# Row scan between two recurrences: norm, way in and way back with channels on partitions

## What is computed

```python
def _L1_ffn_ref(x, W, V, gamma, beta):      # R1, and R2 with its own weights
    Wx = jnp.einsum('bti,hi->bth', x, W)
    ...
    def step(yt, wx_t):
        yt = jax.nn.sigmoid(wx_t + yt @ Vt)
        return (yt, yt)
def _L2_conv_ref(x, W):                     # SC
    rows = jnp.moveaxis(x, 1, 0)
    row0 = rows[0]
    def step(carry, row):
        new = row + jax.nn.relu(conv1d_same(carry, W))
        return (new, new)
    ...
t = t + _L1_ffn_ref(_ln_t(t), L1_ffn_W, ...)
x = x + _L2_conv_ref(_ln_c(x), L2_conv_W)
t = t + _L2_ffn_ref(_ln_t(t), L2_ffn_W, ...)
```

## Time and profile before

| | us |
|---|---|
| median of 3 runs | 560.86 (560.37 to 563.21) |
| the profiled execution, its own time | 561.55 |
| its span | 559.1 |
| busy PE, PEld | 432.0, 329.5 |
| busy DVE, ACT, POOL | 370.2, 236.3, 226.9 |
| chain that ended last, shares | PE 48%, DVE 37%, ACT 5%, POOL 5% |

### The profile page before, as it was taken

The page is one execution under the profiler, slowest core; times in us unless marked ns, Lnnn a source line. Parts: engine busy times, 40 slices in busy tenths (PEclk is TensorE's granted clock), DMA queues, the critical chain, the costliest instruction groups (busy, mean ns, idle before and its releaser), DMA issues.

```text
span 559.1 us, 8700 instructions
## 1 busy us (share of the span) xinstructions
PE 432.0 (77%) x3066; PEld 329.5 (59%) x3066; DVE 370.2 (66%) x1228; ACT 236.3 (42%) x569; POOL 226.9 (41%) x293
## 2 busy tenths in 40 slices
PE   2788868986897757995589976799589848809996
PEld 2456744663347634994389964498355737606664
DVE  4988597749795696007924477501978498398885
ACT  1497555412774554673510024476379634000000
POOL 2598185004582491000500005000359278029994
PEclk9999999678998998899569997799589996558999
DMA  8300000000000000000000000000000000001223
GB/s 162 79 2 1 1 1 1 1 2 0 1 1 1 2 0 1 1 1 2 0 2 2 1 1 1 1 1 1 2 0 2 1 1 1 1 0 20 38 40 56
DMA packets 34670, 6.03 MB, mean 11 GB/s; under 512 B 33713, under 2 KB 34369, under 8 KB 34626
## 3 DMA queue, kind: packets, MB, share of 16 engines
q1 hardware_dynamic: 34626, 5.46, 5.6%
HBM read 3.36 MB, written 2.10 MB: 10 GB/s over the span
## 4 chain that ended last, share of the span: by engine, by line
PE 48%; DVE 37%; ACT 5%; POOL 5%; issue 2%; DMA 1%; SPq 1%; DVEq 0%; POOLq 0%
PE psum L1360 7%; DVE moments L330 6%; DVE ab L742 6%; PE psum L1122 5%; PE psum L1121 5%; DVE ab L726 4%; PE psum L616 4%; PE psum L461 4%; PE psum L1533 3%; POOL z L392 2%; PE psum L627 2%; PE psum L586 2%; PE psum L1553 2%; PE psum L1538 2%; POOL gate L804 2%
## 5 line engine op out<-in xcount | busy, mean ns | idle before, releaser
L461 PE MATMUL psum<-ident,z 128*128 128x128 f32 x256 | 54.2, 354 | 34.5 <-POOL z L392 31.4
L461 PEld LDWEIGHTS psum<-ident,z 128*128 128x128 f32 x256 | 38.5, 182 | 61.9 <-POOL z L392 43.2
L586 PE MATMUL psum<-wp_L,z_t 64*128 64x320 f32 x384 | 66.1, 473 | 3.4 <-ACT z_t L370 2.1
L330 DVE BATCH_NORM_STATS2 moments<-x_cols 128x6 f32<-128x64 f32 x448 | 61.6, 211 | 0.3
L392 POOL TENSOR_TENSOR z<-z,stats 128x496 f32<-128x496 f32 (+1 forms) x35 | 36.8, 1052 | 58.6 <-DVE z L316 58.6
L370 ACT ACTIVATE z_t<-psum 128x512 f32<-128x512 f32 x56 | 40.0, 719 | 33.5 <-PE psum L461 33.4
L586 PEld LDWEIGHTS psum<-wp_L,z_t 64*128 64x128 f32 x384 | 33.2, 192 | 31.0 <-issue 27.6
L387 POOL MEMSET z<- 128x16 f32 x32 | 4.0, 126 | 112.2 <-DVE z L316 111.8
L1213 ACT ACTIVATE ab<-psum,mv 128x128 f32<-128x128 f32 x108 | 39.7, 368 | 19.0 <-PE psum L1122 8.9
L392 POOL TENSOR_TENSOR z<-x_cols,stats 128x512 f32<-128x512 f32 x21 | 22.0, 1048 | 62.9 <-DVE stats L336 62.5
L1122 PE MATMUL psum<-ab,R_vt 128*128 128x128 f32 x216 | 46.8, 300 | 0.0
(11 more groups left out here) (256 smaller groups left out, 912.9 us busy)
## 6 DMA issues: line engine op xcount, KB each, us to landing
x_cols<-in_x_dram SPq DMA_DIRECT2D x16, 128.0 KB, 2.8
out_dram<-x_cols SPq DMA_DIRECT2D x32, 64.0 KB, 1.9
par<-in_par_dram SPq DMA_DIRECT2D x1, 644.5 KB
w<-in_w_dram SPq DMA_DIRECT2D x4, 64.0 KB, 2.3
w<-in_w_dram SPq DMA_DIRECT2D x1, 256.0 KB, 2.7
mask<-in_mask_dram SPq DMA_DIRECT2D x1, 64.0 KB, 2.8
row<-in_row_dram SPq DMA_DIRECT2D x1, 3.3 KB
w_bias<-in_w_dram SPq DMA_DIRECT2D x1, 8.0 KB, 1.9
```

The costliest lines, as they stand in the source:

```text
L330: m = dve.bn_stats(moments[:, q, k:k + 2, :].rearrange("p k m -> p (k m)"), X4[:, SQ * q + s, g:g + 2, :].rearrange("p g c -> p c g"))
L461: m = pe.transpose(bank(b % 2)[:, k * N:(k + 1) * N], block_of(Z)(4 * b + k), ident[:, :])
L586: m = pe.matmul(bank(slot_bank(s) + h, 2 * 5 * C), ZT[rows, s, :], wp[l][rows, :, :], start=True, stop=True)
```

## The change

V1, V2 as whole-map turns, and the norm of SC in blocks, are gone. `XC` now holds x as (row in group, group, channel) from L0 on, so that a block is one transpose wide; L0 still reads the old order, and writes the new one only after all of it is read (`xb`). `cent` is the 32x32 matrix that subtracts the mean over channels, in four copies.

In R1, 32 transposes of x (`turn_x_pe`) are put between the chain of the batch statistics and the first steps, with copies to `XT` on ACT (four banks) and DVE (four banks). In the 16 steps that count, DVE adds each step's states to `XT` and writes `XS`, which is `XR` with (group, channel) on the partitions. The states are not turned back and L1298 is left out for R1.

After the last step PE forms the centred map with (column modulo 4, channel) on the partitions, in two halves of 16 matmuls; each takes 32 partitions to 32 partitions and 512 columns, four to a bank. ACT squares the banks, PE sums the squares over channels and, after root (ACT) and reciprocal (DVE), spreads the result over the channels again; DVE multiplies and writes `RIN`. The scan is the same. After it, PE turns the scanned rows by 32x32 tiles into the layout of `XS`, DVE adds them in eight instructions, and `rows_back_pe` and `rows_back_act` turn blocks back to `XC` in front of, and beside, the norm of R2. F3 writes its result to `XR`, and SP stores from there. POOL makes two more constants (`to_var`, `from_var`).

```diff
+        def x_of(L):
+            return blocks(L.src).rearrange("p g s c -> p s g c") if L is t0 else by_block(L.src)
...
+            if L is r2:
+                for b in range(Q // 2):
+                    rows_back_act(act, b)
             for u in range(LN_STEPS):
+                if L is r2 and u < Q // 2:
+                    rows_back_act(act, Q // 2 + u)
...
+        XT = SQR[:, :].rearrange("p (s n) -> p s n", s=S)
+        XS = XR[:, :].rearrange("p (s n) -> p s n", s=S)
+        XM = XR[:, :].rearrange("p (s n m) -> p s m n", s=S, m=G)
+        XT_BANKS = [0, 1, 2, 3, 4, 5, 6, 4]
+        BACK_BANKS = [4, 5, 6, 7, 2, 3, 4, 5]
+        def turn_x_pe(pe, b):
+            for s in range(4 * b, 4 * b + 4):
+                m = pe.transpose(bank(XT_BANKS[b])[:, s % 4 * N:(s % 4 + 1) * N], block_of(XC)(s), ident[:, :])
+            m.then_inc(v1.s["ps"], 1)
+        def turn_x_copy(eng, b):
+            eng.wait_ge(v1.s["ps"], v1.at["ps"] + b + 1)
+            dst, src = XT[:, 4 * b:4 * b + 4, :], bank(XT_BANKS[b]).rearrange("p (s n) -> p s n", s=4)
+            if b >= 4:
+                eng.tensor_copy(dst, src).then_inc(v1.s["dve"], 1)
+            else:
+                eng.activation(dst, src, ACT.Copy).then_inc(v1.s["act"], 1)
+        def rows_back_pe(pe, b):
+            pe.wait_ge(sc.s["done"], sc.at["done"] + G * (b // 4 + 1))
+            if b >= 6:
+                pe.wait_ge(v2.s["act"], v2.at["act"] + b - 5)
+            for s in range(4 * b, 4 * b + 4):
+                m = pe.transpose(bank(BACK_BANKS[b])[:, s % 4 * N:(s % 4 + 1) * N], XS[:, s, :], ident[:, :])
+            m.then_inc(v2.s["ps"], 1)
+        def rows_back_act(act, b):
+            act.wait_ge(v2.s["ps"], v2.at["ps"] + b + 1)
+            act.activation(XC[:, b * BANK:(b + 1) * BANK], bank(BACK_BANKS[b]), ACT.Copy)\
+                .then_inc(v2.s["act"], 1)
...
+            if L is r1:
+                turn_x_pe(pe, 0)
+                turn_x_pe(pe, 1)
...
+            if L is r1:
+                turn_x_pe(pe, 2)
+                turn_x_pe(pe, 3)
...
+            if L is r1:
+                for b in (4, 5, 6):
+                    turn_x_pe(pe, b)
...
+                    if L is r1 and r == 0 and k == 2:
+                        pe.wait_ge(v1.s["dve"], v1.at["dve"] + 1)
+                        turn_x_pe(pe, 7)
                     for n, h in enumerate(STREAM_ORDER[r]):
+                        if L is r1 and r == 0 and k < 2:
+                            pe.wait_ge(v1.s["act"], v1.at["act"] + 2 * h + k + 1)
...
+            if L is r1:
+                pe.wait_ge(L.s["x1"], L.at["x1"] + STREAMS * CHUNK)
+                for g in range(G):
+                    scan_turn(pe, 0, g).then_inc(sc.s["zt_ps"], 1)
...
+            if L is r1:
+                for b in range(4, 8):
+                    turn_x_copy(dve, b)
...
+                for k in range(CHUNK):
+                    for h in STREAM_ORDER[1]:
+                        dve.wait_ge(L.s[f"step_y{h}"], L.at[f"step_y{h}"] + WARM + k + 2)
+                        first = h * NS_N * CHUNK + k
+                        dve.tensor_tensor(
+                            XS.rearrange("p s n -> p n s")[:, bass.ds(first, NS_N, CHUNK), :],
+                            XT.rearrange("p s n -> p n s")[:, bass.ds(first, NS_N, CHUNK), :], chunks(Y, k + 1, h), ALU.add)\
+                            .then_inc(L.s["x1"], 1)
...
+        def scan_turn(pe, half, g):
+            rows = slice(g * C, (g + 1) * C)
+            for m in range(G):
+                i = pe.matmul(bank(g)[m * C:(m + 1) * C, :], cent[rows, rows],
+                              XM[rows, half * (S // 2):(half + 1) * (S // 2), m, :], start=True, stop=True)
+            return i
+        def scan_unit(t, half, g):
+            return t[:, (G * half + g) * HALF:(G * half + g + 1) * HALF]
+        def scan_square(act, half, g):
+            return act.activation(scan_unit(Z, half, g), bank(g), ACT.Square)
...
+        def scan_norm_pe(pe):
+            L = sc
+            def variances(half):
+                pe.wait_ge(L.s["zt"], L.at["zt"] + G * (half + 1))
+                if half:
+                    pe.wait_ge(L.s["z"], L.at["z"] + 1)
+                for k in range(G):
+                    for g in range(G):
+                        m = pe.matmul(bank(4)[g * C:(g + 1) * C, 0:N], to_var[:, k * C:(k + 1) * C],
+                                      scan_unit(Z, half, g)[:, k * N:(k + 1) * N], start=(k == 0), stop=(k == G - 1))
+                m.then_inc(L.s["var_ps"], 1)
+            def deviations(half):
+                pe.wait_ge(L.s["rstd"], L.at["rstd"] + half + 1)
+                for k in range(G):
+                    for g in range(G):
+                        if half and k == 0:
+                            pe.wait_ge(L.s["z"], L.at["z"] + g + 1)
+                        rows = slice(g * C, (g + 1) * C)
+                        m = pe.matmul(bank(4 + g)[:, k * N:(k + 1) * N], from_var[rows, k, :, :], VRSTD[rows, half, :],
+                                      start=True, stop=True)
+                        if k == G - 1:
+                            m.then_inc(L.s["rstd_ps"], 1)
+            pe.wait_ge(L.s["w_pool"], L.at["w_pool"] + SCAN_COPIES + 2)
+            variances(0)
+            for g in range(G):
+                pe.wait_ge(L.s["zt"], L.at["zt"] + g + 1)
+                pe.wait_ge(L.s["centred"], L.at["centred"] + g + 1)
+                scan_turn(pe, 1, g).then_inc(L.s["zt_ps"], 1)
+            deviations(0)
+            variances(1)
+            deviations(1)
+        def scan_norm_act(act):
+            L = sc
+            warm_table(act, ACT.Sqrt)
+            def deviation(half):
+                act.wait_ge(L.s["var_ps"], L.at["var_ps"] + half + 1)
+                act.activation(VSTD[:, half, :], bank(4, N), ACT.Sqrt, bias=eps[:, L.eps:L.eps + 1], scale=1.0 / C)\
+                    .then_inc(L.s["std"], 1)
+            deviation(0)
+            for g in range(G):
+                act.wait_ge(L.s["zt_ps"], L.at["zt_ps"] + G + g + 1)
+                scan_square(act, 1, g).then_inc(L.s["zt"], 1)
+            deviation(1)
+            for g in range(G):
+                act.activation(XCENT[1][:, g, :], bank(g), ACT.Copy).then_inc(L.s["centred"], 1)
+        def scan_norm_dve(dve):
+            L = sc
+            for g in range(G):
+                dve.wait_ge(L.s["zt"], L.at["zt"] + g + 1)
+                dve.tensor_copy(XCENT[0][:, g, :], bank(g)).then_inc(L.s["centred"], 1)
+            def inverse(half):
+                dve.wait_ge(L.s["std"], L.at["std"] + half + 1)
+                dve.reciprocal(VRSTD[:, half, :], VSTD[:, half, :]).then_inc(L.s["rstd"], 1)
+            def scale(half, g):
+                dve.wait_ge(L.s["rstd_ps"], L.at["rstd_ps"] + G * half + g + 1)
+                at = (2 * g + half) * HALF
+                dve.tensor_tensor(GATE[:, at:at + HALF], XCENT[half][:, g, :], bank(4 + g), ALU.mult)\
+                    .then_inc(L.s["z"], 1)
+            for half in range(2):
+                inverse(half)
+                for g in range(G):
+                    dve.wait_ge(L.s["centred"], L.at["centred"] + (G + g + 1 if half else G))
+                    scale(half, g)
...
+            def turn_rows(half, m):
+                rows = slice(m * C, (m + 1) * C)
+                for g in range(G):
+                    at = 1 + g * S + half * (S // 2)
+                    i = pe.matmul(bank(m if half else 4 + m)[g * C:(g + 1) * C, :], ident[rows, rows],
+                                  SCN[rows, at:at + S // 2, 1:1 + NB], start=True, stop=True)
+                return i
...
-            for b in range(NB // 4):
-                dve.wait_ge(L.s["y_ps"], L.at["y_ps"] + b + 1)
-                x = XR[:, b * BANK:(b + 1) * BANK]
-                dve.tensor_tensor(x, x, bank(4 + b % 4), ALU.add).then_inc(L.s["done"], 1)
+            for half in range(2):
+                for m in range(G):
+                    dve.wait_ge(L.s["y_ps"], L.at["y_ps"] + G * half + m + 1)
+                    x = XM[:, half * (S // 2):(half + 1) * (S // 2), m, :]
+                    dve.tensor_tensor(x, x, bank(m if half else 4 + m).rearrange("p (s n) -> p s n", n=NB), ALU.add)\
+                        .then_inc(L.s["done"], 1)
...
-            turn_x_copy(dve, v1, 1)
-            ln_dve(dve, sc)
+            scan_norm_dve(dve)
             scan_dve(dve)
-            turn_x_copy(dve, v2, 1)
```

More of the change, by code:

```diff
@@ L247, in build @@
         t1 = stage("L1", "norm last weights ones tri", src=XC, scratch=XR, eps=0, e2=EPS)
-        r1 = stage("R1", "scale last turn rec", "g_ps g_y0 g_y1 g_edge_ps g_edge g_turned", src=XC, eps=1, e2=0.0)
-        v1 = stage("V1", "turn_x", src=XC, dst=XR)
-        sc = stage("SC", "norm last turn", "pads w_dve w_pool conv row0 row1 kept size chk chk_ps flag g_conv g_row0 g_row1 g_turned"
-                   " y_ps done", src=XR, eps=2, e2=0.0)
```

(50 more changed lines are left out.)

165 lines of the change are left out of this document (86 added, 79 removed).

## The result

The changed kernel takes 539.1 us (median of 4 runs, 536.75 to 539.61) where the kernel before took 560.62 beside it: a ratio of 0.960, 95% interval 0.956 to 0.965. The prediction was 544, the range 536 to 552. Measured again later, the ratio was 0.961 (0.957 to 0.965). The profiled execution took 539.38 us, its span is 537.6; the span of before was 559.1, so 21.5 us went, where 17.0 were worked out. Two executions of later runs lie far above the others of their kernel, one of contig (2064.94 us) and one of by_m (544.82); the medians and ratios of these two leave them out, and why they were long was not looked into.

The account below looks back on a forecast made before the run. The prediction saw a row of whole-map steps, none beside another, with TensorE full only in recurrence and scan. Terms -1.0, -13.8 and -2.2 summed to -17.0 from 561.55 us, giving 544 us, range 536 to 552.

Parts of the forecast that it names:

- Recurrence of R1: R1's first recurrence, taking in the transposes of x and the additions of states: -1.0 us, bounds +1.5 and -2.2.
- so I take -1.6: R1's recurrence: clock gain from filling the lull, up to 2.8 us, taken as 1.6 because ScalarE's sigmoids set part of the pace.
- +0.4 for block 7: R1's recurrence: the last block of x's transposes goes between two steps of a full PE, costing 0.4 us.
- +0.2 for blocks 2 and 3: Before R1's second mean: these transposes (0.9 us) stand in PE's queue where it had idled 0.63, costing 0.2 us.
- Way in: From R1's last recurrence step to the scan's first matmul: 17.0 us against 31.75, plus about 1 for half clock, so -13.8.
- I take 1.7: Way in: time for 16 matmuls of 32x32 tiles and 512 columns, between 1.0 all at once and 3.6 four at a time.
- I take 0.6: Way in: VectorE's reciprocal of 128 elements, in us, between a lower bound of 0.24 and 0.8 by slope.
- Way back: From the scan to R2's first statistic: -2.2 us, with eight strided additions at 7.6; bounds -4.9 and -1.6.
- VectorE and GpSimd set its pace, so nothing: R2's norm: ScalarE's four later copies (2.4 us) share it, priced at nothing; a full clock there could give up to 2.
- One tile at a time: Rival: small tiles run in sequence, each turning takes 13.8 us instead of 1.7, whole kernel 586 us; chance 0.05.
- four at a time: Rival: tiles overlap along one direction only, +1.9 us in the first turning and before the flag back, 548; chance 0.12.
- Half clock throughout: Rival: R1 starts slow (+1.6), its six blocks take double (+1.3), the way in pays 2 more, 549 us; chance 0.11.

Follow-up runs that it names:

- contig: Changed kernel with the turned map's view by residue read and written in one piece, not every fourth column (output permuted): 535.4 us, ratio 0.954 to the kernel before.
- by_m: Changed kernel with the sum of map and states kept by residue, read in one piece, new map written every fourth column: 536.6 us, ratio 0.957 to before.
- before_fills: Kernel before with unread identity transposes filling idle TensorE stretches, 28 in R1's batch-statistics lull and 28 before R2's norm: 557.7 us, ratio 0.992.
- adds_after: Changed kernel with all 32 additions of R1's states after the recurrence's last step instead of beside its steps: 550.8 us, ratio 0.980 to the kernel before.
- after_again: Changed kernel run once more without edit, for a second trace: 540.8 us, ratio 0.961 to the kernel before.
- after_fills: Changed kernel with idle identity transposes, 26 in R2's batch-statistics lull and 24 before the scan's first matmul: 535.9 us, ratio 0.955 to the kernel before.

## Why the prediction was right, step by step

**Direction and size.** The mechanism was as forecast, and the time lies in the range. Of the 4.5 us between 17.0 and 21.5, 1.1 lie in R1's recurrence, 1.9 in R2's norm, 1.2 in the scan and 0.3 between R2's aggregate and its recurrence. The two ways came out as summed, within 0.1. The surplus of the recurrence and the norm is the granted clock, as before_fills shows; that of the scan cannot be told from chance.

**Recurrence of R1: -1.0 predicted, -2.1 measured.** The mis-sized term is "so I take -1.6" for the clock. before_fills has 27.0 us against 29.5: the clock is worth 2.5, near the bound of 2.8. ScalarE, named as the reason to take less, did not hold the pace: PE is busy 26.27 of 26.99 us. The +0.4 for block 7 is there: 27.4 with it, 27.0 in before_fills without. The +0.2 for blocks 2 and 3 is not, since from the aggregate to the first matmul it is 4.12 us against 4.23. The additions are hidden (adds_after).

**Way in: -13.8 predicted, -13.9 measured**, and that it is so near is luck. At full clock the sum is 17.9 where it was put at 17.0, and the 1 us added for half clock, which did not fall due in the first trace, covers the difference; in after_again it did fall due, at 1.7. The 0.9 are lost by the step of 16 bytes. All sixteen tiles do run at once, 1.15 us, near the bound of 1.0, but at this step a turning takes 2.07, not the 1.7 of "I take 1.7". More is lost in the second half, where the sum has the last bank turned at 7.9, 1.1 behind the last copy. That bank's eight instructions are two on each of four tiles, 1.07 each, and end at 9.1, 2.2 behind the copy; contig has 1.2. The first reciprocal, 0.94 for "I take 0.6", costs nothing, since it ends at 256.12 and the spread waits for this bank until 257.37; the second adds 0.3. Copies and scalings, at 2.48 for four instead of 2.8, give 0.8 back over their three rounds.

**Way back: -2.2 predicted, -2.1 measured.** Eight additions took 8.0 us, not 7.6, and the turning out 1.15, not 1.7; the two misses cancel. That the additions were nearer the strided row was the right choice, and by_m shows that the write at the step is enough for it.

**R2's norm: priced at nothing, measured -1.9.** The failed step is "VectorE and GpSimd set its pace, so nothing", and one of the prediction's own signs of being wrong came true with it: a change over 1 us in a stage priced at nothing. At half clock PE set the pace. Two matmuls took 2.07 us there in the kernel before where the earlier trace rows have 1.02; ScalarE's copy waited for PE, and VectorE for ScalarE's root behind that copy:

```profile
341.98 2.07 PE L1142 MATMUL psum<-z_t,R_wraw 128*128 128x512 f32 x2
...
344.95 1.03 ACT L370 ACTIVATE z_t<-psum 128x512 f32<-128x512 f32 x1 [1.90 <-PE psum L461]
...
346.09 0.25 DVE L336 RECIPROCAL stats<-stats 128x16 f32<-128x16 f32 x1 [1.69 <-ACT stats L358]
```

before_fills takes 2.4 off by the clock alone. The 2 us that only the range held were the likelier case.

**The scan: priced at nothing, -1.2 in the first trace.** before_fills, whose scan nothing touches, also has 39.9 against 41.0, and after_again 40.6 with the change. This much varies by itself, so no gain is claimed; what a warm start gives is 1.5 (after_fills).

**The rivals.** One tile at a time (13.8 us a turning) and four at a time (3.6) fall with the 2.07 and 1.15 us of the two turnings. Half clock throughout falls for R1, where the clock is 1.00; a part of it is real in the way in of after_again (0.78).

## What to carry to other kernels

When a change puts PE work into a lull, price the stages behind the lull at both clocks, also those that the change does not touch: here that was 4 of 21 us, and bare transposes gave most of it to the kernel before. Small tiles at all sixteen places of the array cost about as much as one full matmul of their columns (1.15 us against 1.02), but a column view with a step of 16 bytes nearly doubles that on PE (2.07), and on VectorE a write at that step costs over half as much again as one in one piece (7.58 against 4.87 us). Put filling work ahead of a wait or a branch, never between it and the work that the others wait for.

## What the runs showed of the hardware

- A 32x32 turning of every fourth float takes the same 2.07 to 2.09 us at a clock of 1.00 and of 0.50; in one piece it takes 1.15 at 1.00, where a matmul lasts 0.587 us (1.058 at 0.50, in by_m). The Trainium skill has SBUF lines of 16 bytes, with full rate only from two hits to a line (SBUF — State Buffer, "Specifications (TRN2)"); every fourth fp32 is one hit to a line, and the near doubling agrees with that.
- Sixteen 32x32 tiles run beside each other whatever the order of rows and columns: 32 instructions of 0.588 us in 1.15.
- VectorE's additions of 128 elements last 0.38 us each, but 32 in a row take 0.28 each; a reciprocal of 128 elements takes 0.94, where one of 16 takes 0.24.
- The clock of a stage that PE does not fill can differ between two executions of one program: the way in took 17.9 us at 1.00 and 19.6 at a mean of 0.78 (executions of 539.38 and 543.37 us). A second trace of one's own kernel is worth a run.
